# Causal mask of one-head diagonal score units: added by VectorE within its maximum instead of by a product of TensorE

## What is computed

```python
    def _L0_attn_a_ref(x, w_qkv, b_qkv, w_fc, b_fc):
        ...
        scores = jnp.einsum('bnhd,bmd->bhnm', q, k) / jnp.sqrt(jnp.float32(D))
        causal = jnp.triu(jnp.ones((n, n), dtype=bool), k=1)
        scores = jnp.where(causal, -jnp.inf, scores)
        attn = jax.nn.softmax(scores, axis=-1)
        out = jnp.einsum('bhnm,bmd->bnhd', attn, v)
        ...
    def _L0_attn_b_ref(x, Wq, Wk, Wv, Wo):
        ...
        scores = jnp.einsum('bhqd,bhkd->bhqk', q, k) / scale
        scores = scores + _alibi_bias(H, Tlen)[None]
        attn = jax.nn.softmax(scores, axis=-1)
        out = jnp.einsum('bhqk,bhkd->bhqd', attn, v)
        ...
```

## Time and profile before

| | us |
|---|---|
| median of the runs | 1051.63 |
| lowest and highest | 1050.88, 1053.87 |
| span of the profiled execution | 1051.1 |
| TensorE, VectorE, ScalarE, GpSimd busy | 997.1, 759.5, 589.0, 410.8 |

### The profile page before, as it was taken

One profiled execution on the slowest core, in us unless ns is written; L12 is line 12 of the kernel. 1 busy time (PEld: TensorE's weight loads), 2 busy tenths in 40 slices (PEclk: granted clock), 3 DMA queues, 4 the chain that ended last, 5 costly groups with the idle time before them and its releaser, 6 DMA issues.

```text
span 1051.1 us, 19787 instructions
## 1 busy us (share of the span) xinstructions
PE 997.1 (95%) x6818; PEld 638.7 (61%) x6818; DVE 759.5 (72%) x1564; ACT 589.0 (56%) x1262; POOL 410.8 (39%) x434
## 2 busy tenths in 40 slices
PE   4899999999999999999999999999999999999998
PEld 3533333433348889988886434343343588899887
DVE  6788888888547686447878888888883558764575
ACT  4525776777764335653344657677777643456432
POOL 3420544322443507725743102323234362274470
PEclk9869999999999999999999999999999999999999
DMA  4721212110114415644249533234401152256351
GB/s 133 193 41 30 47 42 43 39 43 13 28 28 149 142 46 155 188 116 118 79 112 227 107 51 57 50 72 74 76 12 44 42 201 60 73 179 165 119 180 51
DMA packets 66755, 95.23 MB, mean 91 GB/s; under 512 B 19669, under 2 KB 50821, under 8 KB 64599
## 3 DMA queue, kind: packets, MB, share of 16 engines
q1 hardware_dynamic: 46645, 52.54, 18.5%
q10 hardware_dynamic: 13100, 22.53, 8.8%
q0 software_dynamic: 6912, 18.88, 7.0%
HBM read 66.59 MB, written 26.67 MB: 89 GB/s over the span
## 4 chain that ended last, share of the span: by engine, by line
PE 74%; DVE 13%; ACT 4%; DMA 3%; issue 3%; POOL 2%; SPq 1%; ACTq 0%; DVEq 0%; POOLq 0%
PE o_ps L1055 14%; PE st_ps L1037 11%; PE su_ps L996 7%; PE st_ps L245 7%; PE st_ps L246 7%; PE st_ps L247 6%; DVE mab L1677 4%; PE st_ps L996 3%; PE o_ps L1195 3%; PE su_ps L1195 3%; PE su_ps L1101 2%; ACT pt L1403 2%; PE st_ps L1230 2%; PE su_ps L1000 2%; DVE xn L1561 1%
## 5 line engine op out<-in xcount | busy, mean ns | idle before, releaser
L1403 ACT ACTIVATE pt<-st_ps 128x512 f32<-128x512 f32 (+3 forms) x768 | 329.0, 495 | 174.4 <-PE st_ps L1037 117.4
L1037 PE MATMUL st_ps<-qs,ks 99*128 99x512 bf16 (+9 forms) x768 | 245.0, 332 | 9.6 <-ACT pt L1403 7.0
L760 POOL TENSOR_SCALAR_AFFINE_SELECT pt<-pt 128x512 f32<-128x512 f32 x120 | 76.2, 635 | 351.5 <-ACT pt L1403 351.5
L1677 DVE TENSOR_REDUCE mab<-su_ps 128x1 f32<-128x512 f32 (+3 forms) x302 | 190.0, 659 | 23.4 <-PE su_ps L1000 16.2
L996 PE MATMUL su_ps<-ks,qs 102*128 102x512 bf16 (+7 forms) x538 | 162.3, 331 | 4.7 <-DVE mc L1677 2.7
L1055 PE MATMUL o_ps<-pt,vp 128*32 128x512 f32 (+3 forms) x1536 | 163.7, 501 | 1.9 <-POOL pt L760 1.0
L1037 PEld LDWEIGHTS st_ps<-qs,ks 99*128 99x128 bf16 (+2 forms) x768 | 73.7, 98 | 116.0 <-ACT pt L1403 65.0
L841 POOL DMA_INDIRECT rows_in<-rows,source x80 | 79.0, 987 | 97.5 <-DVE source L1937 73.7
L1677 DVE TENSOR_REDUCE mab<-st_ps 128x1 f32<-128x512 f32 (+2 forms) x152 | 100.2, 660 | 13.7 <-PE st_ps L1000 10.6
L1429 ACT CAST hh<-hf 128x512 fp32r<-128x512 f32 x64 | 39.7, 621 | 124.4 <-DVE hf L1892 124.4
L996 PEld LDWEIGHTS su_ps<-ks,qs 96*128 96x128 bf16 (+1 forms) x538 | 52.8, 99 | 84.0 <-DVE mab L1677 48.5
(11 more groups left out here) (230 smaller groups left out, 2031.4 us busy)
## 6 DMA issues: line engine op xcount, KB each, us to landing
wu_raw<-w_units_dram SPq DMA_DIRECT2D x32, 384.0 KB, 3.2
outs<-rows_out ACTq DMA_DIRECT2D x40, 256.0 KB, 2.7
q_parts<-hml SPq DMA_DIRECT2D x16, 384.0 KB, 3.4
wexp_raw<-w_units_dram SPq DMA_DIRECT2D x16, 384.0 KB, 7.2
inv<-inverses SPq DMA_DIRECT2D x128, 32.0 KB, 1.8
rows<-xn SPq DMA_DIRECT2D x8, 512.0 KB, 6.6
qs<-q_parts ACTq DMA_DIRECT2D x10, 384.0 KB
k_parts<-hml SPq DMA_DIRECT2D x8, 384.0 KB, 2.5
```

The source lines that it names most:

```text
L760: pool.affine_select(block, block, [[0, 4], [1, P]], ALU.is_ge, 0.0, base=0, channel_multiplier=-1).then_inc(masked, 1)
L1037: last = pe.matmul(bank[KM_BANKS[n % len(KM_BANKS)]][:, lo - CH * part:hi - CH * part], key_stack(l, s)(j)[0:rows, P * kt:P * kt + P], que ...
L1403: act.activation(exponentials(s, q, lo, hi)[:, j, :], bank[KM_BANKS[i % len(KM_BANKS)]][:, lo - CH * part:hi - CH * part], ACT.Exp, scale= ...
L1677: dve.tensor_reduce(to, bank[SU_BANKS[n % len(SU_BANKS)]][:, 0:share * width].rearrange("p (j k) -> p j k", j=share), AX.X, ALU.max).then_ ...
```

## The change

Three things change.

- In diagonal units with one head (384 and 512 keys wide; 16 of a step's 38) TensorE no longer adds the mask. `by_matmul` tells which units still have it: those with 4 or 2 heads, 6 units with 16 mask products in a step.
- In the 16 units VectorE's maximum becomes `tensor_tensor_reduce`: it adds a constant to the bank and takes the maximum in one pass. The constant, `later_keys`, is 512 columns of float32, zero but for the mask in the last 128; a narrower unit reads its last columns. The sum is written to one of two buffers in SBUF, `unread0` and `unread1`, which nothing reads. A wait (`added_before`) keeps a buffer from being written before the unit two of these earlier is done.
- The constants are laid out anew: 8 tables of 128 columns instead of 5.

```diff
+LEAST = -3e38
...
+def by_matmul(u):
+
+    _, _, _, share, _, diagonal = SU[u]
+    return diagonal and share > 1
...
+ADDED = [u for u in range(len(SU)) if SU[u][5] and not by_matmul(u)]
+
+
+def added_before(S, u):
+
+    at = ADDED.index(u) - 2
+    if at >= 0:
+        return unit_base(S) + ADDED[at] + 1
+    return unit_base(S - 1) + ADDED[at] + 1 if S else 0
...
-        cst = sb("cst", [P, 5, P], F32)
-        before_it, all_ones = cst[:, 3, :], cst[:, 4, :]
-        ident = cst[:, 0, :]
+        cst = sb("cst", [P, 8, P], F32)
+        later_keys = cst[:, 0:4, :].rearrange("p a m -> p (a m)")
+        ident, before_it, all_ones = cst[:, 4, :], cst[:, 6, :], cst[:, 7, :]
...
+        unread = [nc.alloc_sbuf_tensor_at(f"unread{n}", [P, CH], F32, offset=base[1] + (28 + 2 * n) * kb) for n in range(2)]
...
-                                     start=True, stop=not diagonal)
-                    if diagonal:
+                                     start=True, stop=not by_matmul(u))
+                    if by_matmul(u):
                         last = pe.matmul(out_b[:, c0 + width - P:c0 + width], identb, mask_q, start=False, stop=True)
...
-                dve.tensor_reduce(to, bank[SU_BANKS[n % len(SU_BANKS)]][:, 0:share * width].rearrange("p (j k) -> p j k", j=share),
-                                  AX.X, ALU.max).then_inc(su_used, 1)
+                src = bank[SU_BANKS[n % len(SU_BANKS)]][:, 0:share * width]
+                if diagonal and not by_matmul(u):
+                    wait(dve, su_used, added_before(S, u))
+                    dve.tensor_tensor_reduce(unread[ADDED.index(u) % 2][:, 0:width], src, later_keys[:, CH - width:CH], 1.0, LEAST, ALU.add, ALU.max, to).then_inc(su_used, 1)
+                else:
+                    dve.tensor_reduce(to, src.rearrange("p (j k) -> p j k", j=share), AX.X, ALU.max).then_inc(su_used, 1)
```

More of the change, by code:

```diff
@@ L281, in program @@
         mhalf = sb("mhalf", [P, TC], F32)
-        cst = sb("cst", [P, 5, P], F32)
-        before_it, all_ones = cst[:, 3, :], cst[:, 4, :]
-        ident = cst[:, 0, :]
+        cst = sb("cst", [P, 8, P], F32)
+        later_keys = cst[:, 0:4, :].rearrange("p a m -> p (a m)")
+        ident, before_it, all_ones = cst[:, 4, :], cst[:, 6, :], cst[:, 7, :]
         cstb = sb("cstb", [P, 3, P], BF16)
-        identb, mask_q, mask_k = cstb[:, 0, :], cstb[:, 1, :], cstb[:, 2, :]
+        mask_q, identb, mask_k = cstb[:, 0, :], cstb[:, 1, :], cstb[:, 2, :]
         bias_a = sb("bias_a", [P, 3], F32)
@@ L975, in query_major @@
             def query_major(l, s, u):
-                qt, half, j0, share, width, diagonal = SU[u]
+                qt, half, j0, share, width, _ = SU[u]
                 n = unit_base(step_no(l, s)) + u
@@ L1524, in _ @@
             act.wait_ge(const_in, 16)
-            act.copy(cstb[:, :, :], cst[:, 0:3, :]).then_inc(const_ready, 1)
+            act.copy(cstb[:, :, :], cst[:, 3:6, :]).then_inc(const_ready, 1)
             act.wait_ge(const_ready, 1)
@@ L1666, in maximum @@
             def maximum(l, s, u):
-                qt, half, j0, share, width, _ = SU[u]
+                qt, half, j0, share, width, diagonal = SU[u]
                 S = step_no(l, s)
@@ L2063, in shape_constants @@
     p = np.arange(P)
-    c = np.zeros((P, 5, P), np.float32)
-    c[p, 0, p] = 1
-    c[:, 1, :] = np.where(p[None, :] > p[:, None], NEG, 0)
-    c[:, 2, :] = np.where(p[:, None] > p[None, :], NEG, 0)
-    c[:, 3, :] = p[:, None] < p[None, :]
-    c[:, 4, :] = 1
+    c = np.zeros((P, 8, P), np.float32)
+    c[:, 3, :] = np.where(p[None, :] > p[:, None], NEG, 0)
+    c[p, 4, p] = 1
+    c[:, 5, :] = np.where(p[:, None] > p[None, :], NEG, 0)
+    c[:, 6, :] = p[:, None] < p[None, :]
+    c[:, 7, :] = 1
     slope = (0.5 ** (np.arange(1, H + 1, dtype=np.float32) * 8.0 / H)).astype(np.float32)
```

## The result

| | before | after |
|---|---|---|
| median of the runs, us | 1051.26 | 1045.42 |
| lowest and highest | 1050.33, 1053.87 | 1044.74, 1047.07 |
| span of the profiled execution | 1051.1 | 1044.3 |

The ratio is 0.9938, with a 95% interval of 0.9921 to 0.9955: the changed kernel is faster by about 0.6%. I had said 1052 us and no change that shows, and the time lies 0.1 us under the range.

A forecast was written before the change was run, and what follows sets the result against it. TensorE was taken to bound the kernel, VectorE close behind, in series within each period. Terms of -0.35 and +0.32 us a period, twelve times, gave -0.4, plus 0.4 outside: 0.0, so 1052 us, range 1045.5 to 1061 us.

The forecast's parts named there:

- Two parts in series, one TensorE's, one VectorE's: Each attention period of 29.7 us: about 26.97 us that TensorE rules, then 2.77 us that VectorE rules.
- Nine masks at 0.06 us: In TensorE's part of a period, nine of the removed mask products save 0.06 us each, 0.54 us.
- Four masks lost ahead of ScalarE: Four of 13 removed products in TensorE's part only bring TensorE sooner to a wait for ScalarE: 0 saved.
- Three masks in VectorE's part save nothing: Three of a period's 16 removed products lie where TensorE waits for VectorE anyway: 0 saved.
- The addition, 0.08 us a unit: On VectorE, each one-head unit's addition with maximum plus write-out costs 0.08 us more than the reduction it replaces.
- The two bank stalls, 0.13 and 0.06: In TensorE's part, a weight load at 198.34 and a product at 209.63 wait for VectorE's maxima: 0.13 and 0.06 us.
- The end of the period, +0.32: In VectorE's part, the last four maxima each cost 0.08 us more: +0.32 us a period.
- Outside the periods, +0.4: Mostly ahead of layer 0's first step: additions +0.64, +0.32, +0.32 against masks saved, -0.85; in all +0.4 us.
- Nothing for the constants, the unread buffers and GpSimd's contention with the pair: Larger constants, the wait for the unread buffer, and GpSimd beside the addition and write-out each counted as 0.
- Rival 2: TensorE keeps nearly all it is spared, no bank stalls, addition 0.06 us: -0.54 us a period, 1045 us, chance 0.20.
- Rivals 1 and 3: Write-out waits: 0.16 us a unit, 1060 us (chance 0.30); addition at half rate: 1095 to 1148 us (chance 0.04).

The follow-up runs named there:

- the spaced kernel with the rest in PSUM: Changed kernel plus one 8-element VectorE maximum ahead of each addition, rest between the turned maxima's parts kept in their PSUM bank: 1052.82 us, ratio to before 1.0001.
- the kernel before with the rest in PSUM: Kernel before, all masks on TensorE, with only the rest between the turned maxima's parts moved from SBUF into their PSUM bank: 1052.47 us, ratio 0.9997.
- e7_back_tail: Changed kernel with mask product and plain reduction put back in the last three 512-wide units of the eighth query tile: ratio to before 0.9946, period 29.22 us.
- the spaced kernels: Changed kernel with one or two 8-element VectorE maxima ahead of each addition: 1056.58 us, ratio to before 1.0031, with one; 1063.5 us, 1.0095, with two.

## Why the prediction was wrong

Step by step, as it was put:

- **Two parts in series, one TensorE's, one VectorE's.** Right. From the turning product (183.15) to the first 512-wide diagonal maximum (209.53) it is now 26.38 us, and from there to the next turning product 2.79. The same two stretches before were 27.00 and 2.74 (186.14, 213.14, 215.88): -0.62 and +0.05.
- **Nine masks at 0.06 us.** Right to the hundredth: four of them put back cost 0.24. The first part as a whole fell by 0.62, the nine with the next item's 0.06 give 0.60; but 0.09 of the fall goes with the hold, so the parts don't add up exactly.
- **Four masks lost ahead of ScalarE.** Nearly right. I counted 0, four at about that place were worth 0.06 together.
- **Three masks in VectorE's part save nothing.** Right, by the second period of layer 0 (29.14 us with them, 29.17 without). In the regular ones 0.08 us go with the hold by GpSimd.
- **The addition, 0.08 us a unit.** This is the step that failed. It is 0.01. The lower bound, 0.06, was itself too high, because I took it for certain that a second instruction occupies at least the distance at which a tiny one follows another. The write-out takes almost no time of its own: the next instruction starts together with it. No row of before could show it, but I had also no row that excluded 0, so the bound should have been there.
- **The two bank stalls, 0.13 and 0.06.** With 0.01 for the addition the formula gives 0 for both (198.34 + 0.02 - 0.18 = 198.18 against the 198.19 wanted; slack 0.08 + 0.17 - 0.24 = 0.01), and they aren't there. This is the load of the earlier trace rows in the changed kernel, 11.96 us behind the turning product where it was 12.20, thus the full 0.24 us earlier:

```profile
195.11 0.10 PEld L1017 LDWEIGHTS su_ps<-ks,qs 96*128 96x128 bf16 x1 [0.24 <-DVE mab L1703]
```

The load waits for VectorE, 0.24 us, but its product starts at 195.21, 0.22 us behind the one before it (194.99), so TensorE's products have no gap.

- **The same stalls at an addition of the forecast's size.** In the spaced kernel with the rest in PSUM, whose addition is 0.07 us above the changed kernel's and 0.08 above the reduction, the same load comes at 12.10 (200.19 behind 188.09), so the stall there was 0.14, as priced. But the first part of its period is only 0.08 us longer than without the spacing (0.35 for the whole, less 4 x 0.068 at its end). So at an addition of the forecast's own size the two stalls would have been over-priced, at 0.19 for about 0.08: a second step that is off, hidden by the first. I hadn't followed a stall beyond its place; what gives the difference back is probably a later wait for ScalarE, but I didn't separate it.
- **The end of the period, +0.32.** Measured +0.05, by the failed step.
- **Outside the periods, +0.4.** With 0.01 it is 0.16 - 0.85 = -0.7 by the same count; measured were -1.7 up to the first turning product, and +0.34 - 0.1 later. The surplus isn't the change's: the granted clock in 70 to 80 us is 0.66 before and 0.83 after, but it is 0.83 too in the kernel before with the rest in PSUM, which has all its masks and its first turning product at 96.44 us. With 0.66, as before, and nearly all masks gone (`e7_back_tail`) it is at 97.37, 0.4 earlier than before.
- **Nothing for the constants, the unread buffers and GpSimd's contention with the pair.** Right: the first transposition starts at 11.26 us, 0.03 later, and no addition shows a wait other than for TensorE. What I overlooked is that the contention which I quoted for the small instructions would change when GpSimd and VectorE shift against each other: 0.09 us a period.

With the measured 0.01 in place of 0.08, and nothing else changed, the sum reads -0.54 + 0.05 = -0.49 us a period, twelve times -5.9, and -0.7 outside: -6.6 us. The span fell by 6.8, the median by 5.8. That the sum comes so close is partly luck: regular periods fell by 0.57, the twelve together by 5.3, and 1.5 lie outside them, of which 1.3 also come without the change (the first turning product at 96.44 us, above). Where the hold by GpSimd is taken out of both kernels, the period differs by 0.48.

The converse holds in part. The kernel that really has my 0.07 to 0.08 us, undisturbed by the hold, runs at 1.0001 of the time before, and I had forecast no change. But its regular period is 29.52 us, 0.22 under the kernel before, where I had 0.03. In its profile the difference is given back by a first period of 30.39 us at a granted clock of 0.83 and by the one long period, which my sum didn't have. So the number agrees better than the working.

**Rival 2** gave the right time, 1045 us, for reasons of which only a part holds: the two bank stalls did stay away. But it had ScalarE's waits move along with TensorE, which they don't, and an addition of 0.06, at which, by the spaced kernels, a good part of the gain would be gone. Rivals 1 and 3 needed additions that aren't there. With the slot at 0.75 us (two tiny instructions) the kernel is 0.95% slower, where rival 1 had 0.8% for 0.76, but here too the sum agrees by luck: the regular period is 0.25 us longer than before, not 0.53, and the rest is in long periods.

The sentence on the Trainium skill's rule ("VectorE: DVE Perf Modes", § Two Vector instructions with no wait between them: neither half of the pair is held, since all operands start at the same place) points to the right end, and the trace agrees: neither waits for the other to finish, each addition starts 0.07 us before the one ahead has ended (210.15, where that one ends at 210.22). I gave it no weight beyond "the low end", and the low end was short of the truth.

## What to carry to other kernels

When an edit puts a small unknown price on one engine 16 times a period, and the sum cancels at the price assumed, then the forecast is only that price. A lower bound needs a row that shows it, and without one it is zero. Work taken from the first engine counts by its place: here in full where that engine rules, a quarter ahead of a wait for another, nothing where another engine rules. And when two engines shift against each other, look at what else meets there: here two small VectorE instructions with all operands in SBUF lasted until GpSimd's product was done, and one operand in a free corner of a PSUM bank avoided it.

## What the runs showed of the hardware

- The write-out of a maximum (`DVE_READ_ACCUMULATOR2_ANT`, 0.08 us long) starts together with the next VectorE instruction. The pair takes a slot of 0.613 us for 512 elements, 0.60 for the plain reduction; 0.475 for 384 (99.25 to 100.20, two of them; 0.465 for the reduction) and 0.345 for 256.
- A second tensor in SBUF, 128x512 in float32, read beside one in PSUM, and a written output of 128x512 in SBUF cost VectorE at most the 0.013 us between these two slots. None of the additions lasts over 0.69 us, also beside GpSimd.
- A cast and a subtraction of 32x128 elements, 0.21 and 0.28 us alone, last up to 1.29 and 1.38 us beside GpSimd products of 1.27 us. With one operand in PSUM they take 0.28 each at any time.
- A maximum of 8 elements on VectorE takes a slot of 0.07 to 0.08 us.
- The issue of one transfer by ScalarE (`ks<-k_parts`) took 0.44 us in most periods and up to 1.59 in some. Where it took 1.45, the exponentials behind it started 1.01 us later and the period was 0.9 us longer.
